# Two 64-row matmuls side by side for the experts' down products, with one of their two banks shared with the transposes

## The reference, cut to what matters

```python
probs = sigmoid(x @ router_w.T + expert_bias)        # 160 experts
top_w, top_idx = top_k(probs, 8)                     # 8 for each token
h1  = silu(einsum('th,eih->eti', x, w_gate))         # 128 -> 64 for each expert
h1w = h1 * combine.T[:, :, None]
routed = einsum('eti,ehi->th', h1w, w_down)          # 64 -> 128 for each expert
```

## Time and profile before

| | |
|---|---|
| three runs, median | 2508.86 us (2505.62 to 2515.23) |
| span of the profiled execution, first to last instruction | 2311.0 us |
| its own device time | not listed; only the span is |
| median less span | 197.9 us |
| mean granted TensorE clock | 0.888 |
| PE busy over the span | 1940.2 us |
| DVE busy | 1648.3 us |
| ACT busy | 1311.8 us |
| GpSimd busy | 1499.3 us |
| quads, from the first T to the last Y | 260.1 to 1037 us |

### The profile page before, as it was taken

One profiled execution on the slowest core, in us unless ns is written; L12 is line 12 of the kernel. 1 busy time (PEld: TensorE's weight loads), 2 busy tenths in 40 slices (PEclk: granted clock), 3 DMA queues, 4 the chain that ended last, 5 costly groups with the idle time before them and its releaser, 6 DMA issues. The chain is left out here.

```text
span 2311.0 us, 29708 instructions
## 1 busy us (share of the span) xinstructions
PE 1940.2 (84%) x8440; PEld 871.8 (38%) x8440; DVE 1648.3 (71%) x3485; ACT 1311.8 (57%) x2685; POOL 1499.3 (65%) x1476
## 2 busy tenths in 40 slices
PE   4676499999998998886777688889899889899986
PEld 2343266665655555553333232222222222222221
DVE  4877165664656666566477324999999898999998
ACT  3354154554535455354588556776676676776663
POOL 0388485774355745408652004999999999999997
PEclk9778799999999999998788798898898898888885
DMA  9931387786765755631110004555555555555552
GB/s 379 393 94 58 89 243 216 226 236 194 198 200 166 223 162 160 186 115 50 43 36 20 0 6 110 115 115 117 118 124 120 120 128 129 130 129 126 124 123 45
DMA packets 210968, 321.50 MB, mean 139 GB/s; under 512 B 28914, under 2 KB 102644, under 8 KB 210420
## 3 DMA queue, kind: packets, MB, share of 16 engines
q1 hardware_dynamic: 194420, 286.02, 45.6%
q0 software_dynamic: 16384, 33.59, 5.1%
HBM read 207.29 MB, written 112.20 MB: 138 GB/s over the span
## 5 line engine op out<-in xcount | busy, mean ns | idle before, releaser
L1498 DVE TENSOR_TENSOR_SCAN db<-pa,db 128x512 f32<-128x512 f32 x512 | 596.5, 1205 | 50.4 <-POOL db L1549 33.8
L1549 POOL TENSOR_TENSOR db<-dur,bb 128x1024 f32<-128x1024 f32 x256 | 596.7, 2360 | 45.6 <-DMA dur<-d_scratch 44.3
L1479 ACT ACTIVATE pa<-dlr,an 128x510 f32<-128x510 f32 x512 | 339.8, 681 | 188.8 <-DVE db L1498 188.1
L1022 POOL DMA_INDIRECT yg<-y_disp,idx x256 | 255.5, 998 | 182.7 <-DMA y_disp<-yb 86.5
L725 POOL DMA_INDIRECT x_disp<-xt,idx x256 | 254.4, 994 | 147.8 <-DVE p L699 91.9
L860 ACT ACTIVATE pr<-sm,nbi 128x128 f32<-128x128 f32 (+1 forms) x512 | 228.1, 447 | 205.9 <-DVE nbi L883 204.2
L907 POOL TENSOR_SCALAR pr<-pr,rcp 128x128 f32<-128x128 f32 x320 | 135.9, 435 | 236.0 <-DVE rcp L892 233.7
L1404 PE MATMUL pb<-db,rw_all 128*32 128x512 f32 x1024 | 213.2, 703 | 81.1 <-DVE db L1504 45.4
L883 DVE CUSTOM_DVE_ANT_0 sm<-pa,rw_front 128x128 f32<-128x128 f32 (+1 forms) x512 | 160.9, 351 | 101.1 <-PE pa L780 100.8
L143 ACT ACT_TABLE_LOAD x146 | 187.3, 1283 | 55.8 <-DVE lg L587 16.2
L790 PE MATMUL pb<-rw_all,pr 128*128 128x128 f32 x768 | 144.5, 300 | 75.0 <-DVE ptt L877 47.8
(11 more groups left out here) (292 smaller groups left out, 3374.7 us busy)
## 6 DMA issues: line engine op xcount, KB each, us to landing
wb<-in_wexp SPq DMA_DIRECT2D x576, 96.0 KB
x_disp<-yb SPq DMA_DIRECT2D x8, 4608.0 KB, 30.1
xb<-x_disp SPq DMA_DIRECT2D x144, 256.0 KB
y_disp<-yb SPq DMA_DIRECT2D x144, 256.0 KB
dlr<-d_scratch SPq DMA_DIRECT2D x128, 256.0 KB, 5.2
dur<-d_scratch SPq DMA_DIRECT2D x128, 256.0 KB, 8.2
bb<-bc_scratch SPq DMA_DIRECT2D x64, 256.0 KB
d_scratch<-dl SPq DMA_DIRECT2D x32, 256.0 KB, 4.7
```

Of the source, the lines that this page charges most:

```text
L1022: e.e.indirect_dma_start(out=YG[:, t % 2, j, :], out_offset=None, in_=YD[h], in_offset=bass.IndirectOffsetOnAxis(ap=IDX[:, c:c + 1], axis= ...
L1479: e.e.activation(decay(a).rearrange("p (b l) -> p b l", b=2)[:, :, 1:256], DLR[:, h % 2, i % 4, :].rearrange("p (b l) -> p b l", b=2)[:, : ...
L1498: e.e.tensor_tensor_scan(hk(a), decay(a), hk(a), 0.0, ALU.mult, ALU.add).then_inc(s_scan, 1)
L1549: e.e.tensor_tensor(DB[:, b % ND, :, :], DUR[:, h % 2, 2 * (b % 2):2 * (b % 2) + 2, :], BB[:, b // 2 % 4, :].rearrange("p (o l) -> p o l", ...
```

## The change

The down products of a quad become four matmuls of 64 contraction rows and 128 columns in place of two of 128 rows and 256 columns. The even blocks (r = 0) read partitions 0 to 63 and write the first half of `MB`; the odd ones (r = 1) read partitions 64 to 127 and write the first half of `PB[1]`. The copy to `YB` is made in two parts of 128x256, `PB[1]` first, and the second one raises `s_qy`. New waits keep the users of `PB[1]` apart. D and Y are planned at q + 1.62 and q + 1.8, and for the four quads before a back group (92, 106, 120, 134) behind it, at 0.96 of the next quad. The zero halves of the weights stay in the data and are loaded as before.

```diff
--- before.py
+++ after.py
@@ -57,8 +57,8 @@
  'qgate': 0.8265,
  'qtanh': 1.2037,
  'qstt': 1.2651,
- 'qdown': 1.7277,
- 'qyb': 2.0102,
+ 'qdown': 1.62,
+ 'qyb': 1.8,
  'qout': 2.8324,
  'sum': 10.1825,
  'b_sg': 0.2077,
@@ -909,6 +909,15 @@
                     m.then_inc(s_pnp, 1)
 
 
+        def down(r):
+            return (MB, PB[1])[r][:, 0:256]
+
+        def at_down(q, u):
+
+            if q + 2 in [after(g) for g in range(NH2)]:
+                return at_quad(q + 1, 0.96 + 0.2 * u)
+            return at_quad(q, PL["qdown"] + u)
+
         def sp_experts(e):
             for q in range(NQ):
                 yield at_quad(q, -RQ + PL["qload"])
@@ -945,6 +954,7 @@
                 yield at_quad(q, 0)
                 e.wait_ge(s_q[i], 80 * (q // RQ + 1))
                 e.wait_ge(s_qx, q)
+                e.wait_ge(s_qy, q - 1)
                 e.wait_ge(s_rkb, NG)
                 for g in range(NH2):
                     if q >= after(g):
@@ -971,12 +981,17 @@
         def pe_down(e):
             for q in range(NQ):
                 i = q % RQ
-                yield at_quad(q, PL["qdown"])
+                yield at_down(q, 0)
                 e.wait_ge(s_qm, q + 1)
                 e.wait_ge(s_qy, q)
+                e.wait_ge(s_qx, min(q + 2, NQ))
+                for g in range(NH2):
+                    if q + 2 >= after(g):
+                        e.wait_ge(s_lln, NG + g + 1)
                 for c in range(2):
-                    m = e.e.matmul(MB[:, 256 * c:256 * c + 256], HM[:, q % 2, 128 * c:128 * c + 128],
-                                   WB[:, i, 2 * c:2 * c + 2, 64:192], start=True, stop=True)
+                    for r in range(2):
+                        m = e.e.matmul(down(r)[:, 128 * c:128 * c + 128], HM[64 * r:64 * r + 64, q % 2, 128 * c:128 * c + 128],
+                                       WB[64 * r:64 * r + 64, i, 2 * c + r, 64:192], start=True, stop=True)
                 m.then_inc(s_qd, 1)
 
         def act_experts(e):
@@ -1003,11 +1018,14 @@
 
         def dve_down(e):
             for q in range(NQ):
-                yield at_quad(q, PL["qyb"])
+                yield at_down(q, PL["qyb"] - PL["qdown"])
                 e.wait_ge(s_qd, q + 1)
                 e.wait_ge(s_yo[q % 3], 16 * (q // 3))
                 e.wait_ge(s_k8, NG)
-                e.e.tensor_copy(YB[:, q % 3, :], MB[:, :]).then_inc(s_qy, 1)
+                for r in (1, 0):
+                    m = e.e.tensor_copy(YB[:, q % 3, :].rearrange("p (c r n) -> p r c n", c=2, r=2)[:, r, :, :],
+                                        down(r).rearrange("p (c n) -> p c n", c=2))
+                m.then_inc(s_qy, 1)
 
 
         def pool_back(e):
@@ -1045,6 +1063,7 @@
             for g in range(NG):
                 yield at_back(g, PL["b_sg"])
                 e.wait_ge(s_qx, after(g) if g < NH2 else NQ)
+                e.wait_ge(s_qy, after(g) - 2 if g < NH2 else NQ)
                 e.wait_ge(s_lln, NG + g)
                 e.e.matmul(PB[1][0:64, :], w("wsh")[:, 0:64], of(XN, g), start=True, stop=True).then_inc(s_sg, 1)
                 yield at_back(g, PL["b_cb"])
```

## The result

The changed kernel takes 2579.03 us (2563.44 to 2586.11), before 2512.05 us beside it: a ratio of 1.0247, 95% interval 1.0213 to 1.0282. It is slower by 2.5%, some 62 us, and outside the range that was forecast.

What follows compares the result with a forecast made beforehand. PE was taken to bound the quads. Gain 49 us from D, less 23 (T's stalls), 10 (sums), 4 (back groups) and 4 (D's wait): 8 us, from 2508.9 to 2501 us; 8-in-10 range 2474 to 2536.

Steps and rivals of the forecast that it cites:

- What D gives: Down products on PE: D shrinks from 1.02 to 0.64 us, 0.38 a quad, 49 us gained over 144 quads.
- So PE is what the quads wait for: Reading of the quads' 773 us: PE busy 719, idle 54 (7%), so PE taken as the bound.
- What the copies cost: Y on DVE: two copies take 0.76 us in place of one of 0.69; the 10 us cost nothing on DVE alone.
- T's wait: T on PE waits for Y's copies of the shared bank: 0.33 to 0.46 us stalls, 23 us, plus 10 for sums.
- tight quads: The 65 of 144 quads with G alone between D and the next T on PE: 23 us of stalls.
- D's wait for X: D(q) on PE waits for X(q+1) where D follows T at once: 0.4 us each in some 9 quads, 4 us.
- Moved, but free: D's move to 1.62 starts SP's loads 0.5 us earlier, Y's writes keep their place, GpSimd gets nothing new: no cost.
- At the back groups: D and Y of one quad put between second norm and T: 1 us for each of four, 4 us lost.
- The gathered sums: DVE's 16 sums of gathered rows in the second half; about seven stand just ahead of a Y: 10 us lost.
- The base: Time around the profiled span of 2311.0 us: 197.9 us by the median, taken to stay unchanged.
- The second: DVE is late: Y behind row minima, H, X and sums releases T late; 27 us slower, 2536; chance 0.18.
- Rival 3: D's pairs on PE don't overlap: D stays 1.02 us, nothing gained; 39 us slower, 2548; chance 0.07.

Runs made afterwards that it cites:

- the gate's bank: Before with paired D, second half in the gate products' bank, G, tanh, H and D planned later: 1.0146; control without pairs 1.0269.
- the early release: Changed kernel, but T and the back group wait only for the copy of the shared bank `PB[1]`, not for both copies: 1.0218.
- early places: D and Y planned at 1.62 and 1.8; paired with T released by half 2367.45 us, against 2392.01 unpaired with all waits.
- old places: Changed kernel with D and Y back at 1.7277 and 2.0102, except ahead of back groups: 1.0145; with T released by half 1.0026.
- B: Condition of a set of runs in which the kernel before took 2510 to 2512 us; the changed kernel was measured only here.
- the wide D: Before with the new order and all new waits, but D as two wide matmuls into its own bank, one copy: 2392.01 us, 1.0324.
- A: Condition of a set of runs in which the kernel before took 2317 to 2321 us.
- the order alone: Before with only the new places of D and Y in the plan, no new wait, D still two wide matmuls: 2358.97 us, 1.0182.

## Why the prediction was wrong

It forecast 2501 us, no change, and missed by 78 us. By its own steps:

*What D gives.* D's own price was right: 0.64 us forecast, 610.19 to 610.83 measured, 0.67 on average, 50 us over all quads. That its 0.38 us a quad become 49 us of time is the first step that failed. "So PE is what the quads wait for" was read off busy times; GpSimd's 407 us looked idle enough, while in the scatters of the first half its program ran without a gap. There the saving showed as 1.6 us, and as 12.0 once the scatters were spread (341.7 against 353.7). Over the kernel, compared within one set, the pairs were worth 28 us with the gate's bank, and with the early release 25 us (early places) and 36 us (old places); in the changed kernel itself they have not been priced.

*What the copies cost.* Right in size: 611.30 to 612.05 is 0.75 us, forecast 0.76.

*T's wait.* Of the right size: 33 us forecast for tight quads and sums, 47 measured in B over 68 times, and 26 with the wide D in A. The handover from DVE to PE was taken as 0.05 us from the other direction; the copy ends at 612.05 and T starts at 612.20, so 0.15. Over 65 tight quads that is 6.5 us of the difference.

*D's wait for X.* The second step that failed: forecast 4 us, measured 46 to 55. It took X's end from the earlier trace rows, 1.38 us behind its T, as if X hung on T alone. X stands behind H on DVE, H behind the tanh, the tanh behind exponentials on ACT, and these behind a row minimum. In the turn shown X starts 2.44 us behind T, in the earlier trace rows 0.69.

*"Moved, but free".* The third, and the largest of those that an edit isolates: this paragraph weighs D's move and SP's loads, and the move of Y from 2.01 to 1.80 has no term in the sum at all; that DVE is idle for 304 us was the reason to put the longer copies at nothing. Alone the move of Y costs 2.0%, 46 us by the medians. An engine that idles because it stands before a wait isn't free for what is queued behind that wait. The prediction asked what T would wait for, and not what on DVE would wait behind Y.

*At the back groups* 4 us were forecast; moving D and Y there costs 9 (0.36%), so this was small as said. The gathered sums were named, and not measured alone.

*The clock.* It has no term in the prediction either, which read 1.00 in one window. In the second half of the quads it is 0.97 before, 0.94 with the order alone and 0.90 in the changed kernel.

*The base.* 197.9 us were taken for what lies around a span. They were the difference of two conditions; it shifts no term of the sum, but in B one kernel with the new waits lost 1.2% more than in A (1.0101 against 0.9980), which no row of the first profile could show. The changed kernel's 2.5% is a figure of B.

*The rivals.* The second came nearest: "Behind row minima, H, X and sums it may start 0.4 us later", 27 us slower. It had the engine and the sign right, and the order of the two the wrong way round: the minima stood behind Y, not Y behind the minima. The Trainium skill (TensorEngine Tiling (Array Packing), PSUM Bottleneck) says that tiling speeds up TensorE but not the copying out of PSUM; the traces agree in that D shrank from 1.02 to 0.67 us while the copies take 0.75 in place of 0.69, on the path now. Rival 3 is refuted by D's 0.64.

What the runs settle: with no new wait, Y's early place costs 2.0% (1.4 to 2.6) in B, and the whole order 1.8% in A; the waits cost 33 us on top of it (1.0324 against 1.0182, one set). The pairs take a part of that back, and the changed kernel's 2.5 to 2.9% is what remains. The parts don't add up exactly, since it was measured in B alone. Open is how the waits' part divides between T and D, what the pairs give in the changed kernel, how much of each part is the clock, and why there are two conditions.

## What to carry to other kernels

When an instruction that waits is moved earlier in an in-order engine's program, price what then stands behind it, whether or not the engine has idle time; a copy that nobody waits for belongs behind the work that others wait for. A saving on the busiest engine is worth no more than the next engine's program leaves, and for that its timeline has to be read with the issue gaps, not its busy share. A shared PSUM bank turns two loose steps into links of a loop: walk the loop once through every engine's queue before costing the wait.

## What the runs showed of the hardware

The two matmuls of a pair, 64 rows each and into two banks, started 0.01 us apart in the turn shown, and the four held PE for 0.64 us, 0.67 on average, in place of 1.02. A scatter issued by GpSimd held it for 1.0 us and another 0.17 to 0.30 us before the next instruction, which isn't counted as busy. The same matmuls kept PE busy for 378 us at a mean granted clock of 0.97 and for 393 at 0.94. One and the same program took 2317 to 2321 us in some sets of runs and 2510 to 2512 in others, at a mean granted clock of 0.88 to 0.89 in the first and 0.85 to 0.86 in the second, and a kernel close to it showed there single waits of up to 35 us ahead of an instruction for which the profile has no releaser; I had taken such a gap for time outside the span.
